# Transposing two pairs of 128x512 tiles in 64-row halves inside a decoder layer's attention loop

## The reference, cut to what matters

```python
x = x + attn(layernorm(x), Wq, Wk, Wv, Wo)              # rope(q), rope(k), causal softmax
x = x + xattn(layernorm(x), ctx, pos, pos, Wq, Wkv, Wout, bout)   # axial rope(q), rope(k)
x = x + ffn(layernorm(x), wq_gate, s_gate, wq_up, s_up, wq_down, s_down)

# in attn (and alike in xattn):
q, k = rope(split_heads(x @ Wq.T)), rope(split_heads(x @ Wk.T))
scores = einsum('bhqd,bhkd->bhqk', q, k) / sqrt(dk)
attn = softmax(where(causal, scores, -inf)); ctx = einsum('bhqk,bhkd->bhqd', attn, v)
```

## Time and profile before

| | |
|---|---|
| median of three runs | 1692.16 us (1687.82 to 3995.81) |
| the profiled execution's own time | 1687.21 us |
| its span | 1685.4 us |
| TensorE, share of the span | 97% |
| VectorE, ScalarE, GpSimd | 68%, 58%, 33% |
| mean granted clock of TensorE | 0.996 |
| one turn of the loop | 35.16 us |

### The profile page before, as it was taken

The page is one execution under the profiler, slowest core; times in us unless marked ns, Lnnn a source line. Parts: engine busy times, 40 slices in busy tenths (PEclk is TensorE's granted clock), DMA queues, the critical chain, the costliest instruction groups (busy, mean ns, idle before and its releaser), DMA issues. The chain is left out here.

```text
span 1685.4 us, 40585 instructions
## 1 busy us (share of the span) xinstructions
PE 1641.8 (97%) x14608; PEld 1285.4 (76%) x14608; DVE 1150.1 (68%) x2087; ACT 972.0 (58%) x3817; POOL 552.8 (33%) x535
## 2 busy tenths in 40 slices
PE   6899999999999999999999999998999999999997
PEld 4677777777777777777777777766888888888885
DVE  7777778777787777877778787777744344344332
ACT  6577777777777777777677776766522222222221
POOL 4444444444444444444444444431011011011011
PEclk9999999999999999999999999999999999999999
DMA  6011111101110011100111101021520120120110
GB/s 214 29 32 31 36 43 41 30 30 36 42 42 30 30 36 41 43 30 30 36 39 45 30 30 39 19 74 65 174 76 19 56 75 21 54 75 23 52 50 26
DMA packets 55097, 80.98 MB, mean 48 GB/s; under 512 B 4880, under 2 KB 25488, under 8 KB 55056
## 3 DMA queue, kind: packets, MB, share of 16 engines
q1 hardware_dynamic: 55056, 80.43, 14.6%
HBM read 63.63 MB, written 16.78 MB: 48 GB/s over the span
## 5 line engine op out<-in xcount | busy, mean ns | idle before, releaser
L877 ACT ACTIVATE prob<-bank,nmax 128x128 f32<-128x128 f32 x1536 | 541.3, 408 | 151.0 <-DVE nmax L1099 148.1
L877 ACT ACTIVATION_READ_ACCUMULATOR prob<-bank,nmax 128x1 f32 x1536 | 380.2, 248 | 0.0
L1099 DVE TENSOR_REDUCE nmax<-bank 128x4 f32<-128x512 f32 x376 | 233.5, 683 | 71.4 <-PE bank L536 70.7
L1505 PE MATMUL fbank<-shared,piece_hi 128*128 128x512 f32 x1152 | 280.3, 394 | 0.0
L1505 PEld LDWEIGHTS fbank<-shared,piece_hi 128*128 128x128 f32 x1152 | 215.8, 187 | 53.2
L399 POOL TENSOR_TENSOR rope_buf<-rope_buf 128x512 f32<-128x512 f32 x128 | 168.0, 1323 | 175.6 <-DVE rope_buf L1052 175.5
L1657 DVE SCALAR_TENSOR_TENSOR h<-fbank,su_c,sil 128x512 f32<-128x512 f32 x88 | 65.9, 749 | 198.4 <-PE fbank L1505 197.0
L1591 ACT ACTIVATE sil<-fbank,sg_c 128x512 f32<-128x512 f32 x88 | 60.6, 688 | 173.1 <-PE fbank L1505 172.0
L449 POOL TENSOR_TENSOR cn_l<-cn,cn_h 128x512 fp32r<-128x512 f32 x64 | 82.9, 1296 | 230.2 <-DVE cn L1091 230.2
L1597 ACT ACTIVATE h_h<-h 128x512 fp32r<-128x512 f32 x88 | 55.6, 632 | 175.0 <-DVE h L1657 175.0
L512 PE MATMUL bank<-shared,z1T_h 128*128 128x512 f32 x520 | 140.3, 411 | 4.3 <-ACT shared L860 2.6
(11 more groups left out here) (171 smaller groups left out, 3127.4 us busy)
## 6 DMA issues: line engine op xcount, KB each, us to landing
xA<-in_x SPq DMA_DIRECT2D x32, 256.0 KB, 2.9
xB<-in_x SPq DMA_DIRECT2D x32, 256.0 KB, 2.8
x_scratch<-x SPq DMA_DIRECT2D x32, 256.0 KB, 2.0
shared_loaded<-x_scratch SPq DMA_DIRECT2D x8, 1024.0 KB, 7.8
xr<-x_scratch SPq DMA_DIRECT2D x8, 1024.0 KB, 5.6
out<-xr SPq DMA_DIRECT2D x8, 1024.0 KB, 4.3
cx<-in_ctx SPq DMA_DIRECT2D x32, 128.0 KB, 2.2
range_window<-in_wg SPq DMA_DIRECT2D x27, 112.0 KB, 2.0
```

The lines of the kernel that those rows point to most:

```text
L877: last = nc.scalar.activation(prob[:, c, i, :], S[c][:, i * P:(i + 1) * P], ACT.Exp, bias=nmax[:, c, i:i + 1], accum_out=rs[:, h:h + 1])
L1099: nc.vector.tensor_reduce(out=nmax[:, c, :], in_=S[c][:, :].rearrange("p (g k) -> p g k", g=G), op=ALU.max, axis=AX, negate=True).then_inc ...
L1505: last = nc.tensor.matmul(dst[:, :], w[:, k, cols], z[:, k, :], start=(n == 0), stop=(n == len(passes) * KT - 1))
```

## The change

The two keys `k2` and `k1` are transposed as a pair of tiles in 64-row halves, in two sweeps, as the probabilities are; and so are `z2` and `z1`. In a turn that has probabilities "2b", the sweeps of the keys are woven with theirs: keys first, pair 0 first, keys second, pair 1 first, pair 0 second, pair 1 second. Before the keys' first sweep TensorE waits for both rotated keys. Before the sweeps of z2 and z1 it waits for both inputs and for both banks to be copied; nothing stands between their two sweeps but the wait. One semaphore (`halves_d`) counts all first sweeps, eight in a turn of the loop by the code's count: three sets of two, the keys and the z. The last turn after the loop has no `z1`, and there `z2` is transposed whole as before. The other engines' code is unchanged.

```diff
-        cross_d = {n: sem(f"prob{n}T_first_quarters_done") for n in (1, 2)}
+        halves_d = sem("first_halves_transposed")
...
+            def halves_of_two(tiles, swap):
+
+                for j in range(KT):
+                    last = []
+                    for half, rows in enumerate(HALVES):
+                        dst, src = tiles[half ^ swap]
+                        last.append(nc.tensor.transpose(dst[:, j * P + rows.start:j * P + rows.stop],
+                                                        src[rows, j * P:(j + 1) * P], ident[rows, rows]))
+                return last
+
+            def first_halves_of_two(tiles):
+                pe.sem_inc(gate, 1)
+                return first_halves_end(halves_of_two(tiles, 0)[1])
+
+            def second_halves_of_two(tiles, ready):
+
+                pe.wait_ge(halves_d, ready)
+                pe.sem_inc(gate, 1)
+                second, first = halves_of_two(tiles, 1)
+                return first, second
+
+            def transpose_keys_and_probs(sq, cq, nx):
+                keys = ((TC, RA["k2"]), (PA, RA["k1"]))
+                pe.wait_ge(rot["k2"], sq + 1)
+                if is_first(sq):
+                    pe.wait_ge(riT_r[1], 1)
+                pe.wait_ge(rot["k1"], nx + 1)
+                keys_ready = first_halves_of_two(keys)
+                if cq is not None:
+                    ready = [first_halves_of_probs("2b", cq, 0)]
+                k2, k1 = second_halves_of_two(keys, keys_ready)
+                k2.then_inc(rT_d["k2"], 1)
+                k1.then_inc(rT_d["k1"], 1)
+                if cq is not None:
+                    ready.append(first_halves_of_probs("2b", cq, 1))
                     for pair in range(2):
...
+                        second_halves_of_probs("2b", pair, ready[pair])
+
+            def transpose_z2_and_z1(sq, nz):
+                zs = ((TC, z2), (PA, z1))
+                pe.wait_ge(z_r[1], nz + 1)
+                z2_done, z1_done = second_halves_of_two(zs, first_halves_of_two(zs))
+                z2_done.then_inc(zT_d[2], 1)
+                z1_done.then_inc(zT_d[1], 1)
...
                 if has_s:
-                    pe.wait_ge(rot["k2"], sq + 1)
-                    if is_first(sq):
-                        pe.wait_ge(riT_r[1], 1)
-                    transpose4(TC, columns(RA["k2"])).then_inc(rT_d["k2"], 1)
-                if has_n:
-                    pe.wait_ge(rot["k1"], nx + 1)
-                    transpose4(PA, columns(RA["k1"])).then_inc(rT_d["k1"], 1)
-                if has_c:
-                    transpose_prob("2b", cq)
+                    transpose_keys_and_probs(sq, cq, nx)
                 if has_n:
                     project_v1(range(V1_SPLIT, len(V1_STEPS))).then_inc(pj["v1"], 1)
                 if has_s:
                     pe.wait_ge(z_r[2], sq + 1)
                     pe.wait_ge(k2T_c, sq + 1)
+                if has_s and nz is not None:
+                    pe.wait_ge(rT_r["k1"], nx + 1)
+                    transpose_z2_and_z1(sq, nz)
+                elif has_s:
                     transpose4(TC, columns(z2)).then_inc(zT_d[2], 1)
-                if nz is not None:
-                    pe.wait_ge(rT_r["k1"], nx + 1)
-                    transpose_z1(nz, PA)
```

More of the change, by code:

```diff
@@ L539, in scores2 @@
                 last.then_inc(s_done[2], 1)
-            def transpose_prob(u, q):
-                k = kind(u)
-                for swap in range(2):
-                    for pair in range(2):
[L545 to L558, removed]
+            crossed = {"n": 0, "base": 0}
@@ new lines, in first_halves_end, with halves_of_probs @@
+            def first_halves_end(last):
+                last.then_inc(halves_d, 1)
+                crossed["n"] += 1
+                return crossed["base"] + crossed["n"]
+            def halves_of_probs(u, pair, swap):
+                for i in range(G):
+                    for half, rows in enumerate(HALVES):
+                        c = 2 * pair + (half ^ swap)
+                        last = nc.tensor.transpose(S[c][:, i * P + rows.start:i * P + rows.stop],
+                                                   prob[rows, c, i, :], ident[rows, rows])
+                return last
@@ new lines, in first_halves_of_probs, with second_halves_of_probs @@
+            def first_halves_of_probs(u, q, pair):
+                pe.wait_ge(p_r[kind(u)], G * nth(u, q) + 2 * pair + 2)
+                pe.sem_inc(gate, 1)
+                return first_halves_end(halves_of_probs(u, pair, 0))
+            def second_halves_of_probs(u, pair, ready):
+                pe.wait_ge(halves_d, ready)
+                pe.sem_inc(gate, 1)
+                halves_of_probs(u, pair, 1).then_inc(pT_d[kind(u)], 2)
+            def transpose_prob(u, q):
+                ready = [first_halves_of_probs(u, q, pair) for pair in range(2)]
+                for pair in range(2):
+                    second_halves_of_probs(u, pair, ready[pair])
@@ L629, in turn @@
                 has_s, has_c, has_n, has_o = sq is not None, cq is not None, nx is not None, oq is not None
+                in_loop = has_c and not isinstance(cq, int)
+                if in_loop:
+                    crossed["base"], crossed["n"] = crossed["n"] - 2 * LOOP_HALVES + LOOP_HALVES * cq, 0
                 if is_first(nx):
@@ L737, in turn @@
                     pe.wait_ge(k2T_c, sq + 1)
+                if has_s and nz is not None:
+                    pe.wait_ge(rT_r["k1"], nx + 1)
+                    transpose_z2_and_z1(sq, nz)
+                elif has_s:
                     transpose4(TC, columns(z2)).then_inc(zT_d[2], 1)
-                if nz is not None:
-                    pe.wait_ge(rT_r["k1"], nx + 1)
-                    transpose_z1(nz, PA)
+                if in_loop:
+                    assert crossed["n"] == LOOP_HALVES
+                    crossed["base"], crossed["n"] = 0, before["n"] + LOOP_HALVES * (B - 5)
             def transpose_reciprocals(n, q):
@@ L848, in transpose_ffn_head, with turns_of @@
                     last.then_inc(f_zT, 1)
+            LOOP_HALVES = 8
+            before = {"n": 0}
+            @contextmanager
+            def turns_of(a, b):
+                before["n"] = crossed["n"]
+                with pe.Fori(a, b) as c:
+                    yield c
             pe.wait_ge(c_ready, 6)
             transpose_z1(0)
-            schedule(turn, pe.Fori, last)
+            schedule(turn, turns_of, last)
         @block.scalar
```

## The result

Over five runs each, the changed kernel's median is 1699.5 us (1697.38 to 1700.68) against 1690.01 us before; the ratio is 1.0057, 95% interval 1.0043 to 1.007. The forecast was 1696, in 1681 to 1706. The profiled execution took 1698.81 us, 11.6 more than that of before, and its span is 1697.0. Of the 11.6, 10.5 lie ahead of the masks of the last sequence.

The account below looks back on a forecast made before the run. TensorE, busy all 35.16 us of a turn, bounds the loop unless another engine's chain ties. +0.23 and +0.02 a turn, with the outer turns, make +7 on 1687.2: 1694; 2 added for the median: 1696, range 1681 to 1706.

Parts of the forecast that it names:

- the chain to `cn`: From z2's copy through ScalarE and VectorE to `cn`: z2 ready 0.32 later, maxima and what follows 0.23 later.
- The keys' gain: Keys as halves woven with the probabilities on TensorE: 0.26 us a turn gained, bounds 0.20 to 0.33.
- z's switch and sweeps: z2 and z1 at the turn's end: 0.09 to change tile shape, halves starting from 614.70 to 615.56.
- the causal masks at 615.71: TensorE's next work after z's halves at the turn's end: 615.71 with the keys' gain, against 615.83 before.
- a new stall of 0.39 us: At the output projection: TensorE arrives at 621.49 and waits for `cn` until 621.88.
- both its ties: TensorE waits closely on VectorE twice: output projection for `cn` until 621.65, next scores at 628.08 for `probT`, ending 628.03.
- So the 0.23 stays until there: The 0.23 us delay lasts from the maxima to the next scores at 628.08, behind VectorE's copies of `probT`.
- Rival (b): TensorE alone decides, with slack between z2 and `cn`: -0.12 x 28 = -3, 1684 us; chance 0.22.
- (c): Halves pay in full for keys and z, self-waits vanish: -0.65 a turn, -18, 1669 us; chance 0.08.
- (d): The output projection's new stall brings the lower clock each turn: 1.6 a turn, +45, 1732 us; chance 0.03.
- (e): Self-wait nearer 0.5, or k1 late by 0.1 or more: +0.5 a turn, +14, 1701 to 1706 us; chance 0.11.
- (f): Halves of both tiles don't run side by side: +1 us a turn, +28, 1715 to 1720 us; chance 0.01.

Follow-up runs that it names:

- The wait at the turn's end: Kernel before, all tiles whole, with z1's transposes made to wait for TensorE's own z2 transposes: 1707.0 us, ratio 1.0111.
- the one in its middle: Kernel before, with the reciprocals' transposes made to wait for TensorE's own self-attention output: 1692.5 us, ratio 1.0022.
- the moved v1 steps: Changed kernel with the last two steps of the v1 projection moved behind the sweeps of z2 and z1: 1694.16 us, ratio 1.0033.
- the control: Kernel before with three turns written out in each of nine loop rounds on all engines: 1720.58 us, ratio 1.0181.

## Why the prediction was right in its number and not in its cause

The number, 1696 against 1699.5, and +0.25 a turn against +0.32, came out near, and that was luck. On TensorE alone the forecast was -0.26 + 0.14 = -0.12 a turn, and the chain to `cn` was to turn it into +0.23. Measured are -0.30 + 0.14 + 0.49 = +0.33 on TensorE alone, its queue included, and the chain added nothing. The prediction's own sign of being wrong, "`cn` no later against the scores", is what came: 5.82 us from the masks to the output projection, before and after. Its other signs failed too: the copy `z2T_h` starts 0.38 ahead of the masks and not 0.11 behind them, from z's first half to the masks pass 1.50 us and not 1.01, and the wait for `cn` did not grow. It also said that a run can't tell less than about 2% from no change; the interval here is 0.14% to either side. Its steps by themselves:

- The keys' gain: forecast 0.26 (0.20 to 0.33), measured 0.30. The extra wait for k1 (0.02) can't be seen: the first half starts 0.33 behind the last v1 step, as a plain switch does.
- z's switch and sweeps: forecast 0.09 and a first-to-last distance of 0.86, measured 0.09 and 0.86. The bare wait's 0.38 is exact.
- "the causal masks at 615.71", 0.15 behind the last half: this is the step that failed. It is 0.64, and 0.49 of it a turn were not in the sum. I had priced the queue's part at nothing ("The two further register waits a turn stand in TensorE's queue behind work already issued"), and that holds only as long as no own wait stands in front of it. The branch was hidden by the queue's lead; the sum names no cover for it. The wait at the turn's end, the one in its middle, the moved v1 steps, and the turns that end without a taken branch (0.24 and 0.15 instead of 0.64) show it together.
- "a new stall of 0.39 us" at `cn`: in the changed kernel it did not come, since the scores, late for the other reason, held the maxima back first. The chain and both its ties were real: in the run with z1 first they cost 0.24 a turn, and in a turn without a branch the output projection came 0.24 later than in the control.
- "So the 0.23 stays until there": partly wrong. q2's transposes earn 0.13 to 0.14 back, and the tie at `probT` takes 0.12 of it again only when `cn` is 0.32 late.
- Rival (b), TensorE alone decides, is the nearest in kind: TensorE does decide in the changed kernel, but with its queue included, and that turned its -3 us into a loss. Rivals (c), (d), (e) and (f) did not occur: the granted clock stayed at 1.00 through the loop, with gaps of 0.4 us in every turn. Gaps of some us at the branches of the written-out turns did bring the lower clock, as (d) had it for the 2.94 us of start-up. Inside a sweep the halves run 1.75 times as fast as whole tiles. The Trainium skill, TensorEngine Tiling (Array Packing), Theoretical Speedup, has up to 2 for such tiles; unwoven, with the waits that two tiles on two banks need, the trace leaves nothing of it (ratio 0.9993).

The turn's loss explains 8 to 9 of the 10.5 us by which the masks of the last sequence are later (the medians are 9.5 apart). The rest lies in the three start-up turns, 1.5 us in all, the first of which is 0.7 longer (its keys have nothing woven in; forecast 0.5), and in the first looped one, 36.21 us, whose 0.7 above the others is not explained; the last two turns give 0.2 back. What is not shown: why a turn of the control without a branch is down to 34.97, 0.11 to 0.18 below the kernel before. 0.12 of it are there by the second product of the output projection, and a turn ahead of the loop in the kernel before, with no branch either, has 35.03.

## What to carry to other kernels

TensorE's wait for its own work is cheap only with other work between, and dear where its queue's lead hides something: a loop's branch, register steps, a row of waits. (No run here tries it on another engine.) Before adding one, look in the queue's records at what runs ahead there, and count it as path. Halves of tiles paid here only where another pair was woven in, and a pair that ends together delays the one of the two that was wanted first. Half of a change can be a gain: the keys alone are 0.6% faster than the kernel before, while the whole is 0.6% slower.

## What the runs showed that I had not expected

A branch with its register steps takes TensorE's queue about 0.5 us (657.34 to 657.84) and is invisible as long as the queue is ahead. Writing out three turns a round made both kernels slower, by 1.8% for the one before: 121 packets of instructions instead of 27, most of them loaded during the loop, and in each round turns of 37.4 to 38.0, 36.6 and 35.0 us instead of three of 35.15. The first of these has a branch of 3.3 to 3.9 us at its end, and the second runs in part at the lower clock that follows.
